# Mixture-of-experts kernel: the last chunk's experts as sorted blocks instead of dense, rows returned by matmul, start of the block stage reordered

## The reference, cut to what matters

```
x = x + ssm(layernorm(x))            # linear recurrence, 64 complex states
x = x + experts(layernorm(x))        # first pass
x = x + attention(layernorm(x))      # 16 heads of 64, relative bias
x = x + experts(layernorm(x))        # second pass, the stage of this change

def experts(x):                      # 2048 tokens, E = 8, TOP_K = 2, D = 128, H = 256
    xt = x.reshape(-1, D)
    topk_vals, topk_idx = top_k(xt @ router_w.T, 2)
    g = sigmoid(topk_vals); g = g / (g.sum(-1, keepdims=True) + 1e-10)
    out = 0
    for e in range(E):
        ge = sum(where(topk_idx == e, g, 0), axis=-1)
        out += ge[:, None] * ((silu(xt @ w_gate[e]) * (xt @ w_up[e])) @ w_down[e])
    return out
```

## Time and profile before

| | us |
|---|---|
| median of 3 runs | 794.65 |
| lowest, highest | 792.18, 795.33 |
| the profiled execution, its time | 796.53 |
| its span in the trace | 794.5 |
| TensorE busy | 743.0 (94%) |
| VectorE busy | 588.4 (74%) |
| ScalarE busy | 487.2 (61%) |
| GpSimd busy | 363.4 (46%) |

### The profile page before, as it was taken

How to read it: one execution, slowest core, us unless ns; L and a number is a source line. 1 busy time by engine, 2 the same in 40 slices (tenths; PEclk the granted TensorE clock), 3 DMA queues, 4 the chain that set the end, 5 groups by cost and what they waited for, 6 DMA issues and landing times.

```text
span 794.5 us, 13532 instructions
## 1 busy us (share of the span) xinstructions
PE 743.0 (94%) x4251; PEld 510.7 (64%) x4251; DVE 588.4 (74%) x1622; ACT 487.2 (61%) x1118; POOL 363.4 (46%) x414
## 2 busy tenths in 40 slices
PE   4889899998889999999999999999999997978997
PEld 2567688886556666675666675676666663767764
DVE  7898777778799876768867769766989785443376
ACT  6457566655567776775767756767566763444422
POOL 1063899985244444433443424433356764110353
PEclk9999999999999999999999999999999997989999
DMA  9012375463000000000000000040003320031622
GB/s 236 4 40 32 91 131 100 77 257 143 1 2 2 1 1 2 1 1 1 2 1 1 2 2 0 2 126 2 1 11 109 91 80 5 14 100 42 169 56 60
DMA packets 52756, 39.69 MB, mean 50 GB/s; under 512 B 2976, under 2 KB 48704, under 8 KB 52688
## 3 DMA queue, kind: packets, MB, share of 16 engines
q1 hardware_dynamic: 51152, 35.69, 17.3%
q0 software_dynamic: 1536, 3.15, 1.3%
HBM read 31.08 MB, written 7.75 MB: 49 GB/s over the span
## 4 chain that ended last, share of the span: by engine, by line
PE 65%; DVE 15%; issue 9%; ACT 5%; POOL 5%; DMA 1%; SPq 0%; DVEq 0%; POOLq 0%; ACTq 0%
PE psum L1369 13%; PE psum L1351 10%; PE psum L1336 10%; PE psum L309 7%; PE psum L310 5%; PE psum L311 5%; PE psum L577 4%; PE psum L1293 4%; POOL y_rows L978 3%; DVE prob L1476 3%; ACT x_norm L375 1%; POOL hid_lo L804 1%; DVE probT L1483 1%; PE psum L1050 1%; DVE ln_stats L324 1%
## 5 line engine op out<-in xcount | busy, mean ns | idle before, releaser
L1789 POOL TENSOR_SCALAR prob<-prob,ones 128x512 f32<-128x512 f32 x256 | 174.0, 692 | 256.3 <-DVE ones L1465 256.0
L1686 ACT ACTIVATE prob<-prob,ones 128x512 f32<-128x512 f32 x256 | 183.7, 719 | 125.7 <-DVE ones L1476 125.7
L1476 DVE CUSTOM_DVE_ANT_0 prob<-psum,bias_band 128x512 f32<-128x512 f32 x256 | 161.6, 687 | 63.0 <-PE psum L1336 62.0
L1351 PE MATMUL psum<-ident,prob 128*128 128x128 f32 x1024 | 124.2, 273 | 3.0 <-DVE probT L1483 1.9
L1369 PE MATMUL psum<-probT,v 128*64 128x512 f32 x512 | 126.7, 616 | 0.0
L1351 PEld LDWEIGHTS psum<-ident,prob 128*128 128x128 f32 x1024 | 114.6, 141 | 13.6 <-issue 6.2
L804 POOL TENSOR_TENSOR hid_lo<-hid,hid_hi 128x512 fp32r<-128x512 f32 x64 | 94.0, 1487 | 36.4 <-ACT hid_hi L624 36.2
L1483 DVE COPY probT<-psum 128x512 f32<-128x512 f32 x128 | 82.2, 678 | 8.4 <-PE psum L1351 8.4
L1692 ACT COPY probT<-psum 128x512 f32<-128x512 f32 x128 | 74.0, 579 | 2.8 <-PE psum L1351 2.7
L1369 PEld LDWEIGHTS psum<-probT,v 128*64 128x64 f32 x512 | 31.5, 138 | 57.0 <-issue 56.1
L695 DVE TENSOR_TENSOR hid<-hid,gate_all 128x512 f32<-128x512 f32 x56 | 54.4, 976 | 9.8 <-DMA gate_all<-gates 3.1
(11 more groups left out here) (264 smaller groups left out, 1419.9 us busy)
## 6 DMA issues: line engine op xcount, KB each, us to landing
gate_all<-gates SPq DMA_DIRECT2D x28, 256.0 KB, 6.7
bias_band<-bias_rows SPq DMA_DIRECT2D x16, 448.0 KB, 9.0
ys<-y SPq DMA_DIRECT2D x8, 256.0 KB, 4.7
dense_gates<-dense_gates_rows SPq DMA_DIRECT2D x8, 256.0 KB
xs<-x_norm SPq DMA_DIRECT2D x1, 1472.0 KB, 6.8
x_res<-in_x SPq DMA_DIRECT2D x4, 256.0 KB, 5.5
w_raw<-in_w_gate SPq DMA_DIRECT2D x8, 128.0 KB, 3.7
w_raw<-in_w_up SPq DMA_DIRECT2D x8, 128.0 KB, 3.6
```

The lines of the kernel that those rows point to most:

```text
L1351: last = nc.tensor.transpose(bank[turned_home(n) + h][:, j * P:(j + 1) * P], prob[:, n % PROBS, h, j * P:(j + 1) * P], ident[:, :])
L1476: nc.vector.tensor_tensor_reduce(out=prob[:, buf, h, :], in0=bank[scores_home(n) + h][:, :], in1=row_bias, scale=-1.0, scalar=NEG_START, o ...
L1686: nc.scalar.activation(prob[:, buf, h, :], prob[:, buf, h, :], ACT.Exp, bias=peak[:, buf, h:h + 1], scale=-1.0, accum_out=total[:, buf, h: ...
L1789: nc.gpsimd.tensor_scalar(prob[:, buf, h, :], prob[:, buf, h, :], inv[:, buf, h:h + 1], 1.0, ALU.mult, ALU.mult).then_inc(a_n, 1)
```

## The change

It does the following.

- The last chunk becomes group 2 with 15 sorted blocks (53 in all), and its routing has the same functions as the other groups. Everything dense is removed.
- Its rows are 130 wide: 128 features, the token's number in the chunk, and the gate. ScalarE writes the normalised rows once and copies them for the second choice (`last_rows`, `last_rows_again`); VectorE writes the two added columns (`token_rows`, `gate_rows`).
- For each of the 15 blocks VectorE builds a 128x512 matrix from the token number and gate (`block_spread`), ScalarE copies the block's output to SBUF (`block_out`), and TensorE multiplies both into one PSUM bank that collects the chunk (`block_unsort`, four fp32 matmuls of 128 columns). No store and no gather. `last_add` adds that bank to x.
- The register load stands one block ahead (`block_expert`), turn lags two blocks and down three.
- The start is reordered: the silu table is loaded by a small activation before ScalarE's copy of slot 126, `sorted_high(0)` and `sorted_low(0)` stand between the last two copies, blocks 1 and 2 run back to back, and group 1's block table and gates move from the end of attention to blocks 6 and 7.
- Scatters, gathers and combines get other block numbers. The zero fill covers three tensors.

```
-        GROUPS = [(0, 2 * QT), (2 * QT, 3 * QT)]
+        GROUPS = [(0, 2 * QT), (2 * QT, 3 * QT), (3 * QT, 4 * QT)]
+        LAST_G, ROW = 2, D + 2
...
+        def block_expert(pe, i):
+            q, j = BLOCK[i]
+            g, b, n = QUADS[q]
+            if i == FIRST_BLOCK[g]:
+                pe.wait_ge(GS["bd"], g + 1)
+            expert_of[i] = pe.value_load(GRP[g]["bid"].bitcast(I32)[0:1, b + j:b + j + 1], min_val=0, max_val=E - 1)
...
             if j == 0 and q > 0:
-                pe.wait_ge(GS["yc"], q)
+                pe.wait_ge(GS["yc"], min(q, LAST_QUAD0))
+            if i > LAST_BLOCK0:
+                pe.wait_ge(GS["y2"], i - LAST_BLOCK0)
...
+        def last_rows(act):
+            act.wait_ge(LN[3]["rs"], 1)
+            for n in range(QT):
+                tile = (CH - 1) * QT + n
+                last = nc.scalar.activation(rows[:, n, 0, 0:D], x[:, tile, :], ACT.Identity, bias=shift[:, tile:tile + 1],
+                                            scale=rstd[:, tile:tile + 1])
+            last.then_inc(LN[3]["xn"], 1)
...
+        def token_rows(dve):
+            one, pid = iota8[:, 1:2].to_broadcast([P, BANK]), GRP[LAST_G]["pid"]
+            nc.vector.tensor_tensor_scan(token[:, :], one, one, -1.0, ALU.mult, ALU.add)
+            group_link(dve, nc.vector.tensor_reduce(pid, shared["upto"], mybir.AxisListType.X, ALU.add))
+            group_link(dve, nc.vector.tensor_scalar(pid, pid, -1.0, float(P), ALU.mult, ALU.add))
...
+        def block_spread(dve, i):
+            j = i - LAST_BLOCK0
+            dve.wait_ge(GS["ld"][LAST_G], 16)
+            if j >= 3:
+                dve.wait_ge(GS["us"], j - 2)
+            of = xs_in[LAST_G]
+            nc.vector.tensor_scalar(spread_of[:, j % 3, :], token[:, :], of[:, j, D:D + 1], of[:, j, D + 1:D + 2],
+                                    ALU.is_equal, ALU.mult).then_inc(GS["sp"], 1)
+
+        def block_out(act, i):
+            j = i - LAST_BLOCK0
+            act.wait_ge(GS["dn"], i + 1)
+            if j >= 2:
+                act.wait_ge(GS["us"], j - 1)
+            at = BLOCK[i][1] * P
+            nc.scalar.copy(y_last[:, j % 2, :], bank[Y_BANK][:, at:at + P]).then_inc(GS["y2"], 1)
+
+        def block_unsort(pe, i):
+            j = i - LAST_BLOCK0
+            pe.wait_ge(GS["sp"], j + 1)
+            pe.wait_ge(GS["y2"], j + 1)
+            if j == 0:
+                pe.wait_ge(GS["pb"], LAST_G + 1)
+                nc.tensor.matmul(bank[JOB_BANK][:, :], xn[0:1, 3 * QT, :], token[0:1, :], start=True, stop=False,
+                                 skip_group_check=True)
+            for n in range(QT):
+                last = nc.tensor.matmul(bank[JOB_BANK][:, n * P:(n + 1) * P], spread_of[:, j % 3, n * P:(n + 1) * P],
+                                        y_last[:, j % 2, :], start=False, stop=(i == ALL_BLOCKS - 1),
+                                        skip_group_check=True)
+            last.then_inc(GS["us"], 1)
+
+        def silu_table(act):
+            spare = GRP[LAST_G]["spare"]
+            act.wait_ge(a_m, 2 * SLOTS)
+            nc.scalar.activation(spare, iota8[:, 0:1], ACT.Silu)
...
# TensorE, leave
                 sorted_turn(pe, 0)
                 transposes(SLOTS - 1)
+                block_expert(pe, 0)
                 pv(SLOTS - PV_LAG + 1)
-                pe.wait_ge(a_m, 2 * SLOTS)
                 block_gate_up(pe, 0)
+                block_expert(pe, 1)
                 for n in range(SLOTS - QT, SLOTS):
                     pv(n)
+                pe.wait_ge(a_m, 2 * SLOTS)
                 block_gate_up(pe, 1)
+                block_expert(pe, 2)
+                block_gate_up(pe, 2)
+                block_expert(pe, 3)
                 pe.wait_ge(a_ea, SLOTS)
                 pe.wait_ge(a_eb, SLOTS)
                 block_turn(pe, 0)
-                block_gate_up(pe, 2)
+                sorted_turn(pe, 1)
                 pe.wait_ge(GS["pb"], 2)
                 for half in range(2):
                     project_out(B - 1, 1, half)
-                block_turn(pe, 1)
-                sorted_turn(pe, 1)
                 pe.wait_ge(a_o, B * PAIRS)
-                block_down(pe, 0)
                 for i in range(3, ALL_BLOCKS):
                     q, j = BLOCK[i]
                     block_gate_up(pe, i)
-                    block_turn(pe, i - 1)
-                    block_down(pe, i - 2)
+                    if i + 1 < ALL_BLOCKS:
+                        block_expert(pe, i + 1)
+                    block_turn(pe, i - 2)
+                    block_down(pe, i - 3)
                     if j == 1 and q + 1 < len(QUADS):
                         sorted_turn(pe, q + 1)
+                    if i >= LAST_BLOCK0 + 4:
+                        block_unsort(pe, i - 4)
...
+                    if i == 14:
+                        pe.wait_ge(GS["rs"], LAST_G + 1)
+                        group_count(pe, LAST_G, JOB_BANK)
...
# VectorE, steady and leave
                 evacuate(SLOTS - 2)
+                sorted_low(dve, 0)
                 evacuate(SLOTS - 1)
...
+                if i == 5:
+                    token_rows(dve)
+                if i == 6:
+                    group_blocks(dve, 1)
+                if i == 7:
+                    group_weights(dve, 1)
...
+                if i == 13:
+                    group_mask(dve, LAST_G)
                 if i == 14:
-                    group_weights(dve, 2)
+                    group_weights(dve, LAST_G)
                 if i == 15:
-                    dense_pick(dve)
+                    group_start(dve, LAST_G, JOB_BANK)
+                    gate_rows(dve)
+                if i == 16:
+                    group_slots(dve, LAST_G)
+                if i == 17:
+                    group_blocks(dve, LAST_G)
...
                     if j == 2 and q + 1 < len(QUADS):
                         sorted_low(dve, q + 1)
-                    if i >= 2 and BLOCK[i - 2][1] == QUADS[BLOCK[i - 2][0]][2] - 1:
-                        quad_out(dve, BLOCK[i - 2][0])
+                    if 3 <= i < LAST_BLOCK0 + 3 and BLOCK[i - 3][1] == QUADS[BLOCK[i - 3][0]][2] - 1:
+                        quad_out(dve, BLOCK[i - 3][0])
+                    if i >= LAST_BLOCK0 + 2:
+                        block_spread(dve, i - 2)
+                    if i in COMBINE_AT:
+                        combined(*COMBINE_AT[i])
...
# ScalarE, leave
+                silu_table(act)
                 evacuate(SLOTS - 2)
+                sorted_high(act, 0)
                 evacuate(SLOTS - 1)
                 pair_out(B * PAIRS - 2)
-                sorted_high(act, 0)
...
                 for i in range(3, ALL_BLOCKS):
+                    if i >= LAST_BLOCK0 + 4:
+                        block_out(act, i - 4)
                     block_silu(act, i)
-                    block_copy(act, i - 1)
+                    block_copy(act, i - 2)
...
                     if i == 13:
-                        group_exp(act, 2)
+                        group_exp(act, LAST_G)
+                        silu_table(act)
```

More of the change, by code:

```diff
@@ L1136, in dense_down @@
-        def dense_down(pe, e):
-            if e == 0:
-                pe.wait_ge(GS["dg_c"], 1)
-            for h in range(MT):
-                pe.wait_ge(MOE[0]["gm"], DONE2 + 2 * e + h + 1)
-                col = slice(e * MT * D + h * D, e * MT * D + (h + 1) * D)
-                last = nc.tensor.matmul(bank[D_BANK][:, :], ws_down[:, col], d_hid[:, e % 2, h, :],
-                                        start=(e == 0 and h == 0), stop=(h == MT - 1), skip_group_check=True)
-            last.then_inc(MOE[0]["d"], 1)
@@ L1160, in dense_gated @@
-        def dense_gated(dve, e, half):
-            dve.wait_ge(GS["dg_ld"], 16 * E)
-            dve.wait_ge(MOE[0]["mul"], DONE2 + 2 * e + half + 1)
-            buf = d_hid[:, e % 2, half, :]
-            nc.vector.tensor_tensor(buf, buf, d_gate[:, e, :], ALU.mult).then_inc(MOE[0]["gm"], 1)
-        def last_sums(act):
-            act.wait_ge(MOE[0]["d"], STEPS_K + E)
-            for part in range(2):
-                half = slice(2 * P * part, 2 * P * (part + 1))
-                nc.scalar.copy(d_sum[:, half], bank[D_BANK][:, half]).then_inc(MOE[0]["y"], 1)
```

218 lines of the change are left out of this document (75 added, 143 removed).

## The result

| | before | after |
|---|---|---|
| median of 20 runs each, us | 794.55 (790.93 to 796.86) | 796.32 (794.70 to 802.98) |
| profiled execution / its span, us | 796.53 / 794.5 | 795.69 / 793.9 |

The ratio of after to before is 1.0033, 95% interval 1.0019 to 1.0047. The forecast of 787.3 us missed: no gain came (after is 1.8 us slower by the medians), and the time lies 9.0 us above it, inside the range.

What follows compares the result with a forecast made beforehand. TensorE, busy 94% of the span, was taken as the bound. Block 3 at 674.5, plus work 53.9, waits 13.4, last chunk 38.9, end 4.0 and clock 2.5, gave 787.2, stated from the median as 787.3 us; range 780.5 to 798.

Steps and rivals of the forecast that it cites:

- The start: End of attention to block 3: the reordering starts block 3 at 674.5 instead of 683.44, 8.9 us earlier, at full clock.
- One block: Each sorted block on TensorE: 1.38 us of work, with down 0.43 of it and matmul passes at 0.112 each.
- the unsort rival: Last chunk: unsorts run at their weight loads' pace, 0.19 instead of 0.112, 9 us more, 796.5 us; chance 0.04.
- The register load: TensorE's queue: a 0.30 us load, issued one block ahead behind gate and up (0.69), is covered.
- The slower rival: Register load between gate-up and turn becomes the bound: up to 0.3 us a block, 15 us, so 802; chance 0.11.
- The waits of blocks 3 to 37: TensorE waits on VectorE and ScalarE queues at blocks 4, 23, 38 and downs 4, 12, 16, 23, 27, 31: together 13.4 us.
- The last chunk: Fifteen sorted blocks with unsorts replace the dense pass: 38.9 us against 36.7, so 2.2 more.
- the start's gain eaten in the queues: Waits at downs 4 and 12 lower the clock twice, or small VectorE operations run slow: 791 to 795 us; chance 0.17.
- signs of being wrong: Holes before turns or after gate-up; block 3 later than 679; block 38 later than 749; unsorts over 1.2 us.

Runs made afterwards that it cites:

- The new beginning alone: The kernel before with only the change's reordered start, dense last chunk and old lags kept: 787.99 us, ratio to before 0.9931.
- the silu gates: The changed kernel with quad copy and ScalarE end reordered, plus last gates from silu(x)/x instead of exp: 786.24 us, ratio to before 0.9920.
- the two orders together: The changed kernel with VectorE's quad copy ahead of the product and ScalarE's output copies of blocks 49 and 50 ahead of hidden copies: 792.49 us, 0.9988 to before.
- the quad copy first: The changed kernel with VectorE's copy of a quad's outputs ahead of the block's product, not behind product and low part: 791.97 us, 0.9972 to before.

## Why the prediction was wrong

**The start** was right in mechanism and size: 8.9 us from the transposes at the end of attention to block 3, as forecast, and no low clock there. The earlier clock times (block 0's matmuls at 662.8 for 664.35, block 3 at 672.9 for 674.5) are the 1.7 us ahead of it. The new beginning alone gave 8.2 us by the same count, since 0.7 of the 8.9 is work moved behind block 3's start, as the prediction says; of these 8.2, 6.9 were left at the end of the span and 5.5 to 6.5 in medians.

**One block** at 1.38 us was right wherever the queue is full, as are the eight passes of an unsort at 0.9 (782.06 to 782.95 in after), so the unsort rival is out. A block of the last chunk with its unsort takes 2.25 us (2.3 forecast), and the gate matrix, 0.54 us on VectorE, holds none of them. VectorE's small operations took the 0.2 us taken for them (group 1's weights, L957 to L962, 0.16 to 0.20 each).

**The register load** is the step that failed most: "Now it is issued one block ahead, right behind gate and up (0.69), which I take to cover it". In these runs it was covered only where TensorE had matmuls waiting. In and right behind a block with a wait it shows as a hole of 0.2 to 0.35 us ahead of a turn and a block that ends 0.40 to 0.49 us later than without loads. Leaving the loads and the address arithmetic out brought 4.5 us in blocks 3 to 37 and 1.1 in 38 to 51, and a second load cost 0.50 us a block. The size was off too: 0.47 us of sequencer by rows, where the prediction had 0.30. The slower rival named this mechanism with the right sign and a chance of 0.11, but not in its size: on average 4.5 / 35 = 0.13 us a block was bare, not 0.3, and it comes in a few blocks and not in each.

**The waits of blocks 3 to 37** were forecast within a few per cent and nearly one by one: 13.4 in all and 12.6 in the trace (block 4 1.14, down 4 2.74, down 12 4.24, down 16 0.60, block 23 0.95, three downs at 0.61, 0.80 and 0.60, block 38 0.95). The profile puts downs 16, 23 and 31 to ScalarE's hT and not to the quad copy that the prediction names, but they went when that copy moved ahead, so VectorE's order was behind them. What was missing, beside the loads, is time that no row calls a wait. Without any load the same stretch has 63.1 us, of which 6.6 are listed waits: 56.5 where the prediction had 53.9 of work. Most of these 2.6 us stand in two kinds of place of that trace. Blocks 19, 26, 30 and 34, each with the first down of a quad, take 1.82 to 1.96 us instead of 1.38, with hardly any idle listed, since idle counts only from a matmul's modelled end. And at each of the four longest waits the block takes about 0.2 us more than its work and the listed wait. The clock took about 3.1 us instead of 2.5 (low blocks of after against the same blocks with the silu gates), in two places (685 to 688 and 705 to 709). The prediction had left the one behind the 2.74 us wait in the range. Loads are the remainder of after, 75.1 - 56.5 - 12.6 - 3.1 = 2.9, so the 5.3 that were missed are 2.6 unlisted + 2.9 loads + 0.6 clock - 0.8 waits. That split is worked out across two kernels; the loads' part was measured as 4.5, address arithmetic included, where waits are fewer, and the unlisted part would then be smaller here.

**The last chunk** was forecast at 38.9 and took 42.7. The second step that failed is one the sum put at nothing: ScalarE's order at the end, two waits of 0.82 and their restarts, 2.2 us (shown by reordering). Of the remaining 1.6, loads were 1.1 in the kernel without them; down 38 waited 0.83 where 0.7 was forecast, though by the profile for ScalarE's hT and not for VectorE's combines. Even with its end mended the sorted last chunk costs 2.7 us more than the dense pass, near the 2.2 of the prediction, loads and some clock included.

**The rivals.** None had both the time of 796.3 and its reason; the register load's is above. The first (the start's gain eaten in the queues) had 791 to 795 and came nearest. One half of it came true: the clock fell twice, behind downs 4 and 12, but cost 3.1 us and not up to 6.5. The other half, slow small operations on VectorE, did not (0.16 to 0.20 us each). The unsort's rival has the very time, 796.5, and it is out. Of the prediction's own signs of being wrong only one came, the holes before turns: block 38 at 747.95 is short of 749, block 3 and the unsorts were as forecast.

Left open: why the two orders together gave 3.6 us by the ratios where each alone gave 4.8 and 2.4; what the longer lags are worth without the register loads; and how much of what went with the loads is the address arithmetic. None was tried apart.

## What to carry to other kernels

Price an instruction that sits in the bottleneck engine's own queue (a register load, here 0.47 us) as covered only while that queue is full, and count it bare in the block with a wait or the one behind it. A stall costs its length, a restart and perhaps some clock: look for the VectorE and ScalarE queue order that removes it before rebuilding the work. Here the new beginning, two reorderings in the blocks and a silu in place of an exp gave 12 to 13 us, where the rebuilt last chunk cost 2.7. And before taking a gain off two profiles, find a row that stands in the same place of both kernels ahead of the change and count from there: 2.2 of 9.1 us lay ahead of it here.

## What was unexpected of the hardware

- A register load from SBUF costs 0.47 us of TensorE's sequencer by its three rows (0.50 a block by the doubled load), not the 0.302 that its longest instruction shows. The Trainium skill, "DMA: Bandwidth & Descriptors", Latency and other measured facts, has a floor of about 600 ns for the load; the row (302 ns) disagrees, the whole of three instructions comes nearer.
- The clock fell after shorter stalls than the prediction reckoned with. Behind the wait of 2.74 us matmuls ran at 1.2 GHz for 3.1 us (685.2 to 688.3). Waits of 1.6 to 1.8 us were followed by the full level in three kernels with the silu gates (1.00 in every window from 700 to 760 with the silu gates on both orders, with the new beginning and without loads). In three others they were not: with the quad copy first a wait of 1.80 stands in a window of 0.93 (700 to 720), with both orders in one of 0.91 (740 to 760), and with two loads, with another of 0.95 behind it, ahead of or in one of 0.91 (760 to 780). So a forecast of the clock behind a stall under 3 us stays uncertain from these runs.
